# A second accumulator bank in causal attention, and VectorE work regrouped or moved to ScalarE in a linear-attention stage

## The reference

```python
xn = _layernorm(x)
# s: linear attention, 8 heads of 128
q, k, v = xn @ Wq.T, xn @ Wk.T, xn @ Wv.T
o = causal_sum(q, k, v)                  # running state over chunks
z = cumsum(k, axis=1)
denom = maximum(abs(sum(q * z, axis=-1)), 1.0)
o = rmsnorm(o / denom, norm_w)           # per head
s = o @ Wo.T
# f: latent attention, 16 heads of 64, then 8 experts, top 2
h = rmsnorm(xn, g1)
q, c = h @ fWq, h @ Wdkv
k, v = c @ Wuk, c @ Wuv
h2 = xn + softmax(causal(q @ k.T / 8)) @ v @ fWo
t = rmsnorm(h2, g2)
f = h2 + sum_e combine[:, e] * (silu(t @ w1[e]) @ w2[e])
y = x + s * silu(f)
```

## Time and profile before

| What | us |
|---|---|
| Median of the runs (2 runs, 4795.9 to 4796.47) | 4796.19 |
| The profiled execution's own time | 4797.43 |
| Span of its slowest core (core 5) | 4795.8 |
| Spans of the 8 cores | 4777.1 to 4795.8 |
| Linear attention: the 16 chunks, about 434 to 1037 | 603 |
| Causal attention: the 64 blocks, about 1446 to 2532 | 1086 |
| Experts, about 2823 to 4637 | 1814 |
| Final stage, about 4637 to 4796 | 159 |

### The profile page before, as it was taken

One profiled execution on the slowest core, in us unless ns is written; L12 is line 12 of the kernel. 1 busy time (PEld: TensorE's weight loads), 2 busy tenths in 40 slices (PEclk: granted clock), 3 DMA queues, 4 the chain that ended last, 5 costly groups with the idle time before them and its releaser, 6 DMA issues.

```text
span 4795.8 us, 42428 instructions; the slowest of 8 cores (4777.1 to 4795.8 us)
## 1 busy us (share of the span) xinstructions
PE 3125.5 (65%) x13297; PEld 1261.4 (26%) x13297; DVE 1074.9 (22%) x2002; ACT 1071.7 (22%) x1463; POOL 43.7 (1%) x65
## 2 busy tenths in 40 slices
PE   0373333336625666566654449999999999999960
PEld 0132222223201111111111224444444444444420
DVE  4201444420233333333332221111111111111112
ACT  3232111112223333333331111111111111111110
POOL 0000000000000000000000000000000000000000
PEclk9986666668855555555556779999999999999985
DMA  4312000012100000000002130303031211213014
GB/s 150 92 18 40 14 14 14 14 39 37 18 0 1 0 1 0 0 0 1 0 1 57 39 63 1 71 1 71 1 71 20 51 36 36 49 22 71 1 50 161
DMA packets 56027, 158.56 MB, mean 33 GB/s; under 512 B 4224, under 2 KB 5248, under 8 KB 55808
## 3 DMA queue, kind: packets, MB, share of 16 engines
q0 software_dynamic: 39248, 95.54, 10.9%
q1 hardware_dynamic: 16560, 60.30, 3.5%
HBM read 209.42 MB, written 33.55 MB: 51 GB/s over the span
## 4 chain that ended last, share of the span: by engine, by line
PE 61%; DVE 17%; issue 8%; DMA 7%; ACT 6%; DVEq 1%; ACTq 0%; SPq 0%; POOLq 0%
PE pA L157 30%; PE pB L157 23%; PE pw L157 6%; DVE p2lb L937 4%; DMA p4s<-s_sp 2%; PE pt L162 2%; DMA p0x<-x 1%; ACT p2pb L885 1%; PE ps L157 1%; DVE p1o1f L565 1%; DVE p2pb L897 1%; DVE p2omla L943 1%; ACT p2sq L812 1%; DVE p1scm L495 1%; DVE p1o1f L582 1%
## 5 line engine op out<-in xcount | busy, mean ns | idle before, releaser
L157 PE MATMUL pB<-p3w,p3hid 128*128 128x512 bf16 x4096 | 889.2, 379 | 37.8 <-ACTq L96 36.6
L157 PE MATMUL pA<-h3T,p3w 128*128 128x512 bf16 x4096 | 891.9, 380 | 0.0
L1116 ACT ACTIVATE p3hid<-pA 128x512 bf16<-128x512 f32 x512 | 306.2, 598 | 1474.4 <-PE pA L157 1474.4
L157 PE MATMUL pw<-p2pb,p2vaug 128*65 128x512 bf16 x640 | 334.9, 626 | 357.4 <-DVEq L96 357.4
L1138 DVE SCALAR_TENSOR_TENSOR acc<-pB,p3comb,acc 128x512 f32<-128x512 f32 x256 | 192.2, 751 | 1618.6 <-PE pB L157 1618.6
L157 PEld LDWEIGHTS pB<-p3w,p3hid 128*128 128x128 bf16 x4096 | 398.5, 98 | 528.5 <-issue 52.7
L157 PEld LDWEIGHTS pA<-h3T,p3w 128*128 128x128 bf16 x4096 | 401.3, 98 | 485.1 <-issue 3.5
L937 DVE RECIPROCAL p2lb<-ps 64x512 f32<-64x512 f32 x64 | 214.4, 3350 | 208.6 <-PE ps L157 208.6
L885 ACT ACTIVATE p2pb<-pA,p2nmub 128x1024 bf16<-128x1024 f32 x160 | 178.6, 1116 | 334.1 <-PE pA L157 334.1
L157 PEld LDWEIGHTS pw<-p2pb,p2vaug 128*65 128x65 bf16 x640 | 60.1, 144 | 630.3 <-issue 630.3
L162 PE MATMUL pt<-ident,p1o2b 128*128 128x128 bf16 x128 | 16.2, 306 | 290.7 <-DVEq L96 290.7
(11 more groups left out here) (160 smaller groups left out, 1844.7 us busy)
## 6 DMA issues: line engine op xcount, KB each, us to landing
p3w<-w POOLq DMA_DIRECT2D x16, 4096.0 KB, 24.7
p0x<-x SPq DMA_DIRECT2D x16, 512.0 KB, 4.1
xn_sp<-p0xn SPq DMA_DIRECT2D x16, 512.0 KB, 2.9
h_sp<-p0h1b POOLq DMA_DIRECT2D x16, 512.0 KB, 2.9
s_sp<-p1sout SPq DMA_DIRECT2D x16, 512.0 KB, 2.6
p2xnr<-xn_sp SPq DMA_DIRECT2D x16, 512.0 KB, 3.2
p4x<-x SPq DMA_DIRECT2D x16, 512.0 KB, 4.8
p4s<-s_sp SPq DMA_DIRECT2D x16, 512.0 KB, 5.7
```

Of the source, the lines that this page charges most:

```text
L157: t.matmul(o, l, r, start=st, stop=sp), sig=sig)
L1116: e.activation(hv[:, m, :], pb[:, 0:512], AF.Silu), sig=True)
```

## The change

Five edits.

1. In the attention loop the values' accumulator alternates from block to block between the bank `pw` and the bank ps5 (`c.ps[5]`), which this stage did not use; `pvfree` is kept for each of the two. Nothing is reordered.
2. In a chunk of the linear attention the 8 instructions at line 565 become 2, over 512 columns each, with the denominator as an operand that repeats each head's value over 128 columns (`to_broadcast`).
3. The 8 instructions at line 582 become 1 over 1024 columns, in the same way.
4. The copy of pB to `sout` moves from DVE to ACT, and ACT gets a wait for the state's cast (546).
5. In the final stage `gf` becomes two buffers used in turn.

```diff
-            sch.emit("vector", lambda e: e.tensor_copy(state_b[:, :], state_f[:, :]))
+            sch.emit("vector", lambda e: e.tensor_copy(state_b[:, :], state_f[:, :]),
+                     sig=True)
+            sch.wait("scalar", sch.mark("vector"))
...
-        for h in range(AH):
-            pb = c.ps[h // 4]
-            sch.emit("vector", lambda e, h=h, pb=pb:
-                     e.tensor_scalar_mul(o1f[:, 128 * h:128 * (h + 1)],
-                                         pb[:, 128 * (h % 4):128 * (h % 4 + 1)],
-                                         rdn[:, h:h + 1]), sig=(h == AH - 1))
+        for half in range(2):
+            sch.emit("vector", lambda e, half=half:
+                     e.tensor_tensor(
+                         o1f[:, half * 512:(half + 1) * 512].rearrange("p (h t) -> p h t", t=128),
+                         c.ps[half][:, 0:512].rearrange("p (h t) -> p h t", t=128),
+                         rdn[:, half * 4:half * 4 + 4].to_broadcast([128, 4, 128]),
+                         OP.mult), sig=(half == 1))
...
-        for h in range(AH):
-            sch.emit("vector", lambda e, h=h:
-                     e.tensor_scalar_mul(o1f[:, 128 * h:128 * (h + 1)],
-                                         o1f[:, 128 * h:128 * (h + 1)], rst8[:, h:h + 1]))
+        sch.emit("vector", lambda e:
+                 e.tensor_tensor(o1f[:, :].rearrange("p (h t) -> p h t", t=128),
+                                 o1f[:, :].rearrange("p (h t) -> p h t", t=128),
+                                 rst8[:, 0:AH].to_broadcast([128, AH, 128]), OP.mult))
...
-        sch.wait("vector", m_sp_p)
+        sch.wait("scalar", m_sp_p)
         if m_ssp_p is not None:
-            sch.wait("vector", m_ssp_p)
+            sch.wait("scalar", m_ssp_p)
         for sl in range(2):
-            sch.emit("vector", lambda e, sl=sl:
-                     e.tensor_copy(sout[:, sl * 512:(sl + 1) * 512], c.ps[2 + sl][:, 0:512]),
+            sch.emit("scalar", lambda e, sl=sl:
+                     e.copy(sout[:, sl * 512:(sl + 1) * 512], c.ps[2 + sl][:, 0:512]),
                      sig=(sl == 1))
-        sch.certify("vector")
-        m_sout = sch.mark("vector")
+        sch.certify("scalar")
+        m_sout = sch.mark("scalar")
...
+            hpar = hIi[0] % 2
+            hIi[0] += 1
+            oTb = c.pw if hpar == 0 else c.ps[5]
...
-                if p_ == 0 and pvfree[0] is not None:
-                    sch.wait("tensor", pvfree[0])
+                if p_ == 0 and pvfree[hpar] is not None:
+                    sch.wait("tensor", pvfree[hpar])
...
-                    mmi(c, c.pw[0:65, 0:512], vv[:, j, h, 0:65],
+                    mmi(c, oTb[0:65, 0:512], vv[:, j, h, 0:65],
...
-            pvfree[0] = sch.mark("vector")
+            pvfree[hpar] = sch.mark("vector")
...
-    gf = sb("p4g", [128, DM], F32, side="left")
+    gf = [sb(f"p4g{i}", [128, DM], F32, side="left") for i in range(2)]
```

More of the change, by code:

```diff
@@ L860, in p2_mla @@
     pvgate = [None, None]
-    pvfree = [None]
+    pvfree = [None, None]
     bcfree = None
+    hIi = [0]
     for h in range(c.p2_heads):
@@ L927, in p2_mla @@
             sch.wait("scalar", m_pv)
-            sch.emit("scalar", lambda e: e.copy(rlb[64:65, 0:512], c.pw[64:65, 0:512]),
-                     sig=True)
+            sch.emit("scalar", lambda e, oTb=oTb: e.copy(rlb[64:65, 0:512],
+                                                         oTb[64:65, 0:512]), sig=True)
             sch.certify("scalar")
@@ L941, in p2_mla @@
             dsto = omv[pr:pr + 64, m0, I * 512:(I + 1) * 512]
-            sch.emit("vector", lambda e, d=dsto:
-                     e.tensor_tensor(d, c.pw[0:64, 0:512], lb[0:64, 0:512], OP.mult),
+            sch.emit("vector", lambda e, d=dsto, oTb=oTb:
+                     e.tensor_tensor(d, oTb[0:64, 0:512], lb[0:64, 0:512], OP.mult),
                      sig=True)
             sch.certify("vector")
-            pvfree[0] = sch.mark("vector")
+            pvfree[hpar] = sch.mark("vector")
     if c.p2_stage < 7:
@@ L1174, in p4_final @@
         sch.wait("scalar", sch.mark("vector"))
-        sch.emit("scalar", lambda e, i=i:
-                 e.activation(gf[:, :], c.acc[:, i * DM:(i + 1) * DM], AF.Silu), sig=True)
+        sch.emit("scalar", lambda e, i=i, par=par:
+                 e.activation(gf[par][:, :], c.acc[:, i * DM:(i + 1) * DM], AF.Silu),
+                 sig=True)
         sch.certify("scalar")
@@ L1182, in p4_final @@
             sch.wait("vector", prev_y[par])
-        sch.emit("vector", lambda e, par=par: e.tensor_mul(gf[:, :], gf[:, :], sr[par][:, :]))
+        sch.emit("vector", lambda e, par=par: e.tensor_mul(gf[par][:, :], gf[par][:, :],
+                                                           sr[par][:, :]))
         sch.emit("vector", lambda e, par=par: e.tensor_add(yt[par][:, :], xr[par][:, :],
-                                                           gf[:, :]), sig=True)
+                                                           gf[par][:, :]), sig=True)
         m_y = sch.mark("vector")
```

## The result

The changed kernel takes 0.9627 of the time before, with a 95% interval of 0.959 to 0.9664. The profiled execution took 4628.1 us where 4623 was predicted and 4797.4 was the profiled execution before. The spans of its cores are 4606 to 4627 us; the slowest is core 7.

A forecast was written before the change was run, and what follows sets the result against it. Waits, with no engine full, were taken to set the pace in both attention stages, while PE filled the experts' stage. 4797.4 - 111 (causal attention) - 63 (linear attention) = 4623 us; range 4595 to 4672.

The forecast's parts named there:

- Attention, I = 1 to 3: Causal attention, 48 of 64 blocks: first value matmul follows the exponent, not DVE's multiply; 2.31 us each, 111 us saved.
- Attention, I = 0: Causal attention, 16 diagonal blocks: masks still queue behind reciprocal and multiply on DVE, so 0 of 4.55 us saved.
- (a): Linear attention: 8 scalings from PSUM, 3.56 us, become 2 instructions, 1.48 us; 2.08 us a chunk saved.
- (b): Linear attention: 8 scalings in SBUF, 3.11 us, become one instruction of 1225 ns; 1.88 us a chunk saved.
- The rival of a repeated operand at double price: Linear attention: the new wide instructions take twice their time, 43 us more, 4666 us in all; chance 8%.
- (c): Linear attention: moving the copies to `sout` onto ACT is hidden on both engines, 2.1 us to spare; 0 saved.
- the final stage: Final stage: second `gf` releases nothing, as silu waits for earlier DVE work and DVE for loads; 0.
- (d) The clock: Linear attention's Wo projection: a shorter chunk may move PE's clock rise; taken as 0, bounds -7 to +14 us.
- The three allowances: Additions to the forecast time: clock shift up to 14 us, lost ACT cover up to 20, attention block releases 14.
- The attention's gain: Rival in the causal attention: another wait gives its gain back, leaving only 63 us saved, 4734 us; chance 7%.
- The clock did not rise in the attention: Rival in the causal attention: TensorE's clock rises from 0.50, saving 86 us more, 4537 us; chance 8%.
- the slower case: Experts' stage: PE's clock falls below 1.00; at 0.91 the whole gain is lost, at 0.85 4936 us; chance 2%.

The follow-up runs named there:

- the bank alone: The kernel before with only the attention's second accumulator bank added: ratio 0.9774 to the kernel before, 4685.8 us profiled.
- the kernel with masks first: The changed kernel with the previous block's reciprocal and multiply put behind the masks on DVE for 15 blocks with I = 0: 4619.3 us profiled.
- With the old length restored: The changed kernel with three more unused DVE instructions in each linear attention chunk: loop over the chunks 563.8 us; no total time given.
- the pipelined one: The changed kernel with the attention's 64 blocks run as one stream of pairs: ratio 0.9311 to the kernel before, 4468.8 us profiled.
- the wide scalings alone: The kernel before with only both groups of 8 scalings joined into wide instructions: ratio 0.9904 to the kernel before, 4744.0 us profiled.

## Why the prediction was right

**Attention, I = 1 to 3.** Right in size and mechanism: 110.9 us in the stage with the bank alone, 111 worked out; the first value matmul at 3.25 after the spread matmul, 3.22 worked out. The releaser is ACT, as foretold. The step from an ACT end over the no-op to PE, 0.39 us in the earlier trace rows, could be carried over to a wait that did not exist yet, and measured 0.43 there. One reading was off: of the 425 us in 192 places that the prediction gives to the value matmuls, 357.4 us in 176 places are theirs. The sum did not use it.

**Attention, I = 0.** Right: 4.55 us before and after, and the kernel with masks first, where this wait fell to 2.07, shows that DVE's order was the cause.

**Linear attention (a) and (b).** Right in the instructions: 1.49 and 1.23 us against 1.48 and 1.23. The rival of a repeated operand at double price falls with the same rows. The rule of the Trainium skill (VectorE: DVE Perf Modes, The perf-mode tier table), that `tensor_scalar` in f32 between SBUF tiles has twice the rate of `tensor_tensor`, does no harm here. The trace of before agrees in direction (its layer norm has a `tensor_scalar` of 128x1024 f32 at 812 ns, against 1225 ns for a `tensor_tensor` of that size), but eight narrow instructions cost 3.11 us from first to last and one wide one 1.23.

**(c) and the final stage.** Right on the engines: ACT had 2.14 us to spare, 2.1 worked out, and DVE still waits 111.5 us for the loads.

**(d) The clock.** This is the term that was off. I took 0, within bounds of -7 and +14. The Wo projections rose by 5.8 us in the sum and the loop's saving was 5.4 us short of 59.4. About 1 us of that is the wait for DVE (62.3 instead of 63.4); the rest is the clock, Wo dearer and the output matmuls cheaper. With the 1.2 us that the attention fell short, less 1.7 us gained outside both stages, this is the miss of 5 us. The bounds held, in the other kernels too (Wo from 83.8 to 94.3, so -1.5 to +9.0). But the cause I named, the chunk's length, is only part. With the old length restored and the copies on ScalarE the sum stayed at 89.7. And one length gives no one price: the projections drift from chunk to chunk. On core 1 of the kernel before they fall, on core 7 of the changed one they rise (first and fifteenth of 16; rows as in the earlier trace rows):

```profile
469.19 6.48 PE pB L157 x16
...
997.63 5.11 PE pB L157 x16
```

```profile
465.11 5.45 PE pB L157 x16
...
941.73 6.06 PE pB L157 x16
```

What exactly sets the moment of the rise stays open; the runs show only that it moves with the timing of the chunk, and that it differs between cores of one run (81.7 to 86.9 us in the kernel before).

**The range.** The three allowances at the top of the forecast's own range, 14, 20 and 14 us, give 4671 if they all fall together, not 4660. The stated range covers that.

**The other rivals.** The attention's gain was not given back. The clock did not rise in the attention: 0.50 in the changed kernel, and even in the pipelined one, where a stretch of 11 us has PE busy for 10.17. The experts' clock stayed at 1.00, so the slower case did not come. The limit of 13/16 that the prediction takes from the Trainium skill (TensorE: Matmul & The Clock Gate) stands there in the section Seeing it yourself.

## What to carry to other kernels

Where an accumulator is read late by one engine and rewritten early by another, lay the two queues beside each other and work out when each entry could start without the shared bank; the saving is the difference for those passes whose next release is early, and zero for those whose next release stands in the same queue as the old one. Once the bank is doubled, the next gain is in order, not in buffers: issuing the next block's first scores ahead of the end of this one brought another 161 us. Many short VectorE instructions over slices of one tile are worth joining, if they stand on the path: here eight took 3.11 us and one wide one 1.23.

## What the runs showed of the hardware

- TensorE stayed at 0.50 in the attention, where the matmuls use 64 of 128 rows or 65 of 128 columns, also where PE was busy for 12.5 of 15 us (before) and 10.17 of 11 us (pipelined kernel). The Trainium skill (TensorE: Matmul & The Clock Gate, What's actually happening) has sustained activity release the throttle; these stretches do not agree. The Wo projections, with full 128x128 weights, reach the high level before their 16 matmuls are through (a granted clock of 0.70 over one of them on core 1). The runs don't show whether the shape is the reason.
- Shortening DVE's part of a chunk by 3.96 us changed the price of unchanged matmuls: on core 1 the Wo matmuls went from 514 to 561 ns and the output matmuls from 259 to 236 ns with the wide scalings alone. The same 16 matmuls took 6.48 to 4.92 us from chunk to chunk of that core before.
- An f32 operand that repeats one value over 128 columns costs VectorE nothing that can be seen: 692 ns for 512 columns with the other operand in PSUM (688 without repetition), 1225 ns for 1024 from SBUF (1225).
